# Layer 0 rotary embedding: even and odd head dimensions projected to separate tiles, in pairs

## The chip, the cores and the metric

The kernel runs on one core of a Trainium2 chip. The time is the device time of one launch in microseconds (us). TensorE is called PE in the profile (PEld is its weight loads), VectorE is DVE, ScalarE is ACT, GpSimd is POOL and SyncE is SP, which issues nearly all DMAs here.

## What is computed

Two transformer layers over 8 batch entries of 512 tokens by 256 channels. Layer 0 is causal attention with 16 heads of 16 dimensions and rotary position embedding, then a mixture of experts; layer 1 is a windowed attention and a second expert stage. The change touches only the queries and keys of layer 0:

```
q = shape_heads(x @ Wq.T)            # 16 heads of 16 dimensions
k = shape_heads(x @ Wk.T)
_rotate_every_two(x) = stack((-x_odd, x_even), -1).reshape(x.shape)
q = q * cos + _rotate_every_two(q) * sin
k = k * cos + _rotate_every_two(k) * sin
scores = einsum('bhqd,bhkd->bhqk', q, k) * scale      # causal mask, softmax, times v, Wo
```

The frequency of the rotation is the same for the two dimensions of a pair (even, odd), so `cos` and `sin` hold each value twice.

## The kernel before

Layer 0's attention is one function, `layer0_attention` (L246). What each engine does, and in which order, comes from one list of items that `schedule0` (L167) makes: each item is a kind of work, a batch entry `b` and indices, with a time key in units of one group of heads (4 heads; 4 groups to a batch entry, so entry `b` has its groups at 4b to 4b+3). The list is sorted by key, and every engine walks it and does its own kinds in that order; semaphores do the rest. A dictionary `SHIFTED` (L154) moves the keys of single kinds by hundredths of a group, and `front0` (L134) sets other keys for the first two batch entries.

The kinds that matter here:

- `qk` (PE, L395): one tile of a projection, 128 output channels by 512 tokens, from two fp32 chunks of 128 channels (four matmul records a tile). Four tiles of 128 channels hold q and k of a batch entry (i = 0, 1 for q, 2, 3 for k); each is projected twice, with the weights (j = 0) and with weights whose columns are swapped in pairs (j = 1), which gives the rotated partner. So a batch entry has 8 `qk` tiles.
- `rope` (DVE, L638): multiplies one `qk` tile in PSUM by a table (cos for j = 0, signed sin for j = 1) into `halves`, and frees the tile's PSUM bank. 8 a batch entry. `sum` (POOL, L795) adds the two halves.
- `hi` (ACT, L547), `rest` (DVE, L642), `mid` (POOL, L799), `lo` (DVE, L646) split the fp32 sum in three bf16 parts; `park` (SP, L353) writes these to DRAM, and `stack` (SP, L368) reads them back, six DMAs for q and six for k, in the layout in which the scores are made.
- `max` (PE L416 and L419, DVE L653): scores of a part of a group and their row maxima, 11 items a group, in three PSUM banks taken in turn: PE's item n waits until DVE has read item n-3.
- `split` (DVE, L663 to L668), `turn` (PE, L426), `turned` (ACT, L563), `send` (SP, L359): the maxima of a group are transposed and sent into the stacks.
- `exp` (PE L441 and L448, ACT L574): 10 items a group, in two banks. `values` (PE, L465): probabilities times v.
- Once a batch entry: `turn_o`, `norm`, `turn_a`, `out` (PE L499: output projection, two items), `add` (DVE L684), `stats` (DVE L689, L692), `new` (DVE L699), `turn_x` (PE L509), `v` (PE L402), `logit` (L518), `pick`, `rank`, `place`, `scatter` (POOL L815: four indirect DMAs).

`qk`, `turn`, `turn_o`, `turn_a`, `out`, `turn_x`, `v`, `logit` and `rank` share two PSUM banks (`Banks`, called `work`): an item takes the bank that was freed first, as the list has it, and PE waits until its last reader is done. Keys before the change, for entry b with g0 = 4b: tile i is projected at g0 - 7 + i + 0.08 (j = 0) and + 0.25 (j = 1), so each group has two `qk` items and their two `rope`s apart. `out` is at g0 + 5.50 and 5.62, `turn` 0.318 after each group's start, `new` at g0 + 6.06 and 6.24 and `turn_x` at 6.42. Of entry 1 the front has three of the four tiles; the fourth lies after the first maxima. Two `ones` items (DVE L611, L612) fill parts of the stacks before the first maxima.

At the start SP loads `w_qkv` (five blocks of 256 columns: q, k, q swapped, k swapped, v), the first x transposed, the rope table (two sets of channels, cos and sin) and the rest. After layer 0 come `experts` (L822) and layer 1, which start when layer 0 has ended.

Of the kernel before, what the change touches and what calls it, by code (L numbers as in the profile page):

```python
# [12 lines left out]
P = 128  # L13
# [120 lines left out]
def front0():  # L134


    time = {("xt", 1, 0, 0): -8.9, ("stack", 0, 0, 0): -6.52, ("stack", 0, 1, 0): -5.5}
    for i in range(4):
        t = -8 + 0.5 * i
        for j in range(2):  # L140
            time["qk", 0, i, j], time["rope", 0, i, j] = t + 0.2 * j, t + 0.1 + 0.2 * j
        for kind, late in (("sum", 0.35), ("hi", 0.36), ("rest", 0.85), ("mid", 0.9), ("lo", 0.93), ("park", 0.95)):
            time[kind, 0, i, 0] = t + late
        t = (-4.5, -4.0, -3.5, -1.0)[i]
# [10 lines left out]
    "add": {0: -0.032, 1: -0.093}, "exp": {None: -0.088}, "hi": {0: -0.04, 1: -0.079, 2: 0.027, 3: -0.079},  # L155
    "lo": {0: 0.197, 1: 0.34, 2: 0.033, 3: 0.228}, "logit": {None: 0.02}, "new": {0: -0.174, 1: -0.059},
    "norm": {0: -0.02, 1: -0.024, 2: 0.006, 3: -0.055}, "o_in": {None: -0.049}, "park": {2: 0.277},
    "qk": {(0, 0): 0.025, (0, 1): 0.025, (1, 0): 0.025, (1, 1): 0.025, (2, 0): 0.019, (2, 1): 0.08, (3, 0): -0.298, (3, 1): 0.025},
    "rest": {0: 0.006, 1: 0.109, 2: 0.166, 3: 0.2}, "rope": {(0, 0): -0.084, (0, 1): -0.099, (1, 0): -0.07, (3, 1): -0.103},
    "split": {None: 0.054}, "stats": {0: -0.063, 1: -0.067}, "sum": {0: -0.183, 1: -0.128, 2: -0.128, 3: -0.128},  # L160
    "turn": {None: 0.078}, "turn_a": {0: 0.097, 1: 0.024}, "turn_o": {0: 0.024, 1: 0.013, 2: 0.014, 3: -0.024},
# [5 lines left out]
def schedule0():  # L167
# [9 lines left out]
    for b in range(B):  # L177
        g0 = NG * b
        at(g0 - 9, "xt", b)
        for i in range(4):  # L180
            t = g0 - 7 + i
            for j in range(2):
                at(t + 0.08 + 0.17 * j, "qk", b, i, j)
# [1770 lines left out]
```

## Time and profile before

| what | value |
|---|---|
| time, median of 3 runs | 1361.81 us (1360.37 to 1361.99) |
| time of the profiled execution | 1357.76 us |
| its span, first to last instruction | 1356.0 us |
| mean granted TensorE clock | 0.969 |
| busy over the span | PE 1208.0, DVE 929.2, ACT 607.9, POOL 277.0 us |
| `qk` matmul records (L395) | 256, 64 tiles |

The span is the time between the first and the last instruction; what lies around it is 1.8 us here. A busy share is a mean over stages with different limits, so the windows by stage and by group say more. Overlapping records of one engine are merged in a busy time.

### The profile page before, as it was taken

To read this page: it belongs to the slowest core of one execution; us is meant where nothing else is said; L and a number is where in the kernel's file an instruction comes from. 1 tells how busy PE (TensorE), PEld (TensorE's weight loads), DVE (VectorE), ACT (ScalarE), POOL (GpSimd) and SP (SyncE) were. 2 spreads that over 40 slices of the span, in tenths; PEclk is the share of its full clock that TensorE was granted. 3 is DMA by queue.
4 is the path that set the end of the run, shared out by engine and by line. 5 is a ranking of instruction groups with operands and counts; after the bars stand their busy time and mean duration, and the time that the engine had idled before them with its cause. 6 is when DMAs were issued, how large, how long until landed. Compare 5 with 4: busy or idle time off the path is not lost. (4 is left out here: it accounts for less than half of the span.)

```text
span 1356.0 us, 32761 instructions
## 1 busy us (share of the span) xinstructions
PE 1208.0 (89%) x12587; PEld 779.8 (58%) x12641; DVE 929.2 (69%) x2335; ACT 607.9 (45%) x1144; POOL 277.0 (20%) x294
## 2 busy tenths in 40 slices
PE   7589999999999989779999778998989898989865
PEld 3245566655656555449998345555556565655542
DVE  3687767777686766237777668767776768676743
ACT  1044455555454556235554115554545454445441
POOL 3111121212121210111111411222222223212122
PEclk9689999999999999989999888999999999999998
DMA  5443524243342412544221344334251505140000
GB/s 181 129 121 96 148 72 118 80 110 103 87 130 60 130 47 98 186 134 153 71 68 36 95 135 120 98 75 118 57 138 39 148 28 150 38 123 3 19 17 16
DMA packets 68265, 127.88 MB, mean 94 GB/s; under 512 B 8320, under 2 KB 58128, under 8 KB 64656
## 3 DMA queue, kind: packets, MB, share of 16 engines
q1 hardware_dynamic: 65040, 117.38, 31.2%
q0 software_dynamic: 3072, 8.41, 1.9%
q8 instruction: 102, 1.67, 0.5%
q14 instruction: 51, 0.42, 0.1%
HBM read 84.31 MB, written 40.66 MB: 92 GB/s over the span
## 5 line engine op out<-in xcount | busy, mean ns | idle before, releaser
L574 ACT ACTIVATE arena<-pair 128x512 f32<-128x512 f32 x320 | 184.6, 596 | 112.4 <-PE pair L448 107.2
L1511 ACT ACTIVATE second_probs<-pair 128x512 f32<-128x512 f32 (+1 forms) x256 | 135.4, 541 | 195.7 <-PE pair L1373 159.2
L653 DVE TENSOR_REDUCE first_maxima<-bank 128x1 f32<-128x512 f32 (+3 forms) x235 | 146.8, 636 | 55.3 <-PE bank L419 54.5
L1671 DVE TENSOR_REDUCE second_maxima<-bank 128x3 f32<-128x480 f32 (+1 forms) x160 | 105.2, 660 | 58.9 <-PE bank L1340 56.8
L395 PE MATMUL bank<-first_xT,w_qkv 128*128 128x512 f32 x256 | 126.3, 624 | 12.1 <-DMA first_xT<-in_xT 7.9
L441 PE MATMUL pair<-stacks 128*128 128x128 bf16 (+3 forms) x458 | 102.4, 292 | 6.9 <-DMA stacks<-first_m_turned 5.6
L416 PE MATMUL bank<-stacks 96*128 96x512 bf16 (+3 forms) x343 | 87.3, 307 | 14.6 <-DVE first_maxima L653 11.5
L653 DVE TENSOR_REDUCE first_maxima<-pair 128x1 f32<-128x512 f32 (+3 forms) x117 | 74.6, 638 | 25.3 <-PE pair L419 24.8
L1365 PE MATMUL pair<-second_q_stack,second_k_stack 128*32 128x160 bf16 (+4 forms) x2048 | 83.3, 229 | 4.8 <-ACT second_probs L1511 2.8
L448 PE MATMUL pair<-constants_bf 128*128 128x256 bf16 (+1 forms) x320 | 80.7, 252 | 4.3 <-ACT arena L574 1.0
L795 POOL TENSOR_TENSOR first_halves<-first_halves 128x512 f32<-128x512 f32 x32 | 41.5, 1298 | 197.8 <-DVE first_halves L638 197.7
L395 PEld LDWEIGHTS bank<-first_xT,w_qkv 128*128 128x128 f32 x256 | 46.3, 198 | 57.5 <-issue 45.9
L875 PEld LDWEIGHTS pair<-expert_xsT,expert_W_near 128*128 128x128 f32 x624 | 75.5, 192 | 4.7 <-ACT expert_xsT L918 2.9
L875 PE MATMUL pair<-expert_xsT,expert_W_near 128*128 128x128 f32 x624 | 76.4, 276 | 1.8 <-ACT expert_xsT L918 1.8
L465 PE MATMUL pair<-arena,first_values 128*32 128x512 f32 (+3 forms) x1024 | 75.5, 436 | 0.7 <-ACT arena L574 0.7
L907 ACT ACTIVATE expert_W_near<-stacks 128x1024 f32 x39 | 41.1, 1056 | 76.5 <-PE pair L875 60.6
L886 PE MATMUL pair<-stacks,expert_hT 128*128 x312 | 73.9, 380 | 0.6 <-ACT expert_hT L922 0.6
L1365 PEld LDWEIGHTS pair<-second_q_stack,second_k_stack 128*32 128x32 bf16 x2048 | 42.2, 96 | 55.6 <-issue 45.0
L441 PEld LDWEIGHTS pair<-stacks 128*128 128x128 bf16 x512 | 42.3, 98 | 50.9 <-issue 18.2
L638 DVE TENSOR_TENSOR first_halves<-bank,rope 128x512 f32<-128x512 f32 x64 | 43.7, 685 | 34.2 <-PE bank L395 34.0
L1388 PE MATMUL pair<-second_probs,second_values 128*32 128x256 f32 (+1 forms) x1024 | 59.8, 354 | 3.0 <-ACT second_probs L1511 3.0
L886 PEld LDWEIGHTS pair<-stacks,expert_hT 128*128 128x128 f32 x312 | 56.2, 190 | 7.0 <-issue 1.0
(344 smaller groups left out, 2583.1 us busy)
## 6 DMA issues: line engine op xcount, KB each, us to landing
stacks<-parked SPq DMA_DIRECT2D x96, 256.0 KB, 5.2
parked<-first_parts SPq DMA_DIRECT2D x32, 384.0 KB, 2.8
second_q_stack<-parked SPq DMA_DIRECT2D x48, 256.0 KB, 5.0
second_k_stack<-parked SPq DMA_DIRECT2D x48, 256.0 KB, 8.2
parked<-second_parts SPq DMA_DIRECT2D x30, 384.0 KB, 2.6
expert_xs<-sorted_x SPq DMA_DIRECT2D x39, 128.5 KB, 2.1
sorted_y<-expert_ys SPq DMA_DIRECT2D x39, 128.0 KB, 1.7
first_xT<-in_xT SPq DMA_DIRECT2D x8, 512.0 KB
```

The lines of the kernel that those rows point to most:

```text
L395: ins = pe.matmul(bank[:, :], w["qkv0"][:, c, lo:lo + P], xT[b % 2][:, c, :], start=(c == 0), stop=(c == KC - 1))
L416: pe.matmul(mx[n % 3][:, x * wide:(x + 1) * wide], q[0:ROWS, i * GH + hh, qt * P:(qt + 1) * P], k[0:ROWS, i * GH + hh, 0:wide], start=(x = ...
L441: pe.matmul(ex[n % 2][:, lo:lo + wide], k[:, i * GH + hh, kt * P:(kt + 1) * P], q[:, i * GH + hh, kt * P:S], start=(lo == 0), stop=True, s ...
L448: ins = pe.matmul(o, m["idb"][:, :], spread(m["mT0"][:, :], P, len(heads) * len(tiles)), start=False, stop=True, skip_group_check=True)
L465: ins = pe.matmul(pv[VW * hh:VW * (hh + 1), kt * P:S], V[b % 2][:, kt, i * GH + hh, :], PT[:, slot(b, i, hh), lo:lo + S - kt * P], start=( ...
L574: act.activation(PT[:, s:s + len(heads), lo:lo + each], ex[n % 2][:, 0:len(heads) * each].rearrange("p (h q) -> p h q", h=len(heads)), ACT ...
L653: dve.tensor_reduce(nm[:, i, qt, heads[0]:heads[0] + len(heads)], mx[n % 3][:, 0:wide].rearrange("p (h k) -> p h k", h=len(heads)), AX.X, ...
L875: last = pe.matmul(pair[0][:, (j % 2) * F + n * P:(j % 2) * F + (n + 1) * P], near[:, j % 2, c, n * P:(n + 1) * P], xsT[:, j % 2, c * P:(c ...
L886: last = pe.matmul(pair[1][:, (j % 2) * F:(j % 2) * F + D], hT[:, j % 2, c, :], W2[:, c, bass.ts(e, D)], start=(c == 0), stop=(c == FC - 1))
L1365: pe.matmul(ex[n % 2][s * SUB:(s + 1) * SUB, lo:lo + wide], k[:, h, k0:k0 + SUB], q[:, h, k0:k0 + wide], start=(y == 0), stop=True, skip_g ...
L1511: act.activation(PT[:, s:s + len(heads), lo:lo + each], scores[:, :, 0:each], ACT.Exp, scale=SCALE).then_inc(lp["exps"], 1)
L1671: dve.tensor_reduce(nm[:, i, :, :].rearrange("p t h -> p (t h)")[:, first:end], mx[n % 2][:, 0:(end - first) * wide].rearrange("p (u k) -> ...
```

## The change

Weights are ordered so that the even dimensions of all heads (128 channels) make one tile and the odd dimensions the other. A pair of tiles, E and O, gives both rotated halves: E cos - O sin and O cos + E sin. The swapped projections go: `w_qkv` has three blocks instead of five, the rope table is half as large, and a batch entry has four `qk` tiles, not eight. The number of `rope`, `sum`, `hi`, `rest`, `mid`, `lo`, `park` and `stack` items stays. Each tile is now read by two `rope`s; the banks of a pair are freed by the third and fourth `rope` of the pair, which are in the order E cos, O sin, E sin, O cos. Pairs stand at g0 - 6.7 (q) and g0 - 4.7 (k), that is in every second group; the first `sum` chain of a pair follows it, the second is 0.6 of a group later. All `SHIFTED` entries of `qk`, `rope`, `sum`, `hi`, `rest`, `lo` and `park` are dropped. In the front both pairs of entry 1 lie ahead of the first maxima.

```diff
-    for i in range(4):
-        t = -8 + 0.5 * i
...
+    for p in range(2):
+        t = -8 + 0.75 * p
+        for n in range(2):
+            time["qk", 0, 2 * p + n, 0] = t + 0.1 * n - 0.15 * p
+            for j in range(2):
+                time["rope", 0, 2 * p + n, j] = t + 0.2 + 0.1 * n + 0.04 * (j if n == 0 else 1 - j)
...
+        t = (-4.4, -3.3)[p]
...
-        for i in range(4):
-            t = g0 - 7 + i
-            for j in range(2):
-                at(t + 0.08 + 0.17 * j, "qk", b, i, j)
-            for j in range(2):
-                at(t + 0.21 + 0.17 * j, "rope", b, i, j)
-            for n, kind in enumerate(("sum", "hi", "rest", "mid", "lo", "park")):
-                at(t + 0.44 + 0.09 * n, kind, b, i)
+        for p in range(2):
+            t = g0 - 6.7 + 2 * p
+            for n in range(2):
+                at(t + 0.04 * n, "qk", b, 2 * p + n)
+                for j in range(2):
+                    at(t + 0.08 + 0.06 * n + 0.03 * (j if n == 0 else 1 - j), "rope", b, 2 * p + n, j)
+                for q, kind in enumerate(("sum", "hi", "rest", "mid", "lo", "park")):
+                    at(t + 0.21 + 0.6 * n + 0.09 * q, kind, b, 2 * p + n)
...
         if kind == "rope":
-            return [("qk", b, i, j)]
+            return [("qk", b, i - j, 0)] if i % 2 else []
...
-                        dve.wait_ge(lp["qk_ps"], 2 * k + j + 1)
-                        if k >= 2 and j == 0:
+                        of = i ^ j
+                        dve.wait_ge(lp["qk_ps"], 4 * b + of + 1)
+                        if k >= 2:
                             dve.wait_ge(lp["lo"], k - 1)
-                        bank, before = work["qk", b, i, j]
-                        dve.tensor_tensor(halves[:, k % 2, j, :], wk[bank][:, :], w["rope"][:, i % 2, j, :], ALU.mult)\
-                            .then_inc(read[bank], 1)
+                        bank, before = work["qk", b, of, 0]
+                        dve.tensor_tensor(halves[:, k % 2, j, :], wk[bank][:, :], w["rope"][:, j, :], ALU.mult)\
+                            .then_inc(read[bank] if i % 2 else lp["roped"], 1)
...
-                        is_read(pool, ("qk", b, i, 0))
-                        is_read(pool, ("qk", b, i, 1))
-                        pool.tensor_tensor(halves[:, k % 2, 0, :], halves[:, k % 2, 0, :], halves[:, k % 2, 1, :], ALU.add)\
+                        if i % 2:
+                            is_read(pool, ("qk", b, i - 1, 0))
+                            is_read(pool, ("qk", b, i, 0))
+                        else:
+                            pool.wait_ge(lp["roped"], k + 2)
+                        pool.tensor_tensor(halves[:, k % 2, 0, :], halves[:, k % 2, 0, :], halves[:, k % 2, 1, :],
+                                           ALU.add if i % 2 else ALU.subtract)\
...
-                w = {"qkv0": si("w_qkv0", [P, KC, 5 * D]), "o0": si("w_o0", [P, KC, D]), "rope": si("rope", [P, 2, 2, S]),
+                w = {"qkv0": si("w_qkv0", [P, KC, 3 * D]), "o0": si("w_o0", [P, KC, D]), "rope": si("rope", [P, 2, S]),
```

## Rows read from the trace of the kernel before

**Rows 1.** Windows: length, busy us (count) of PE, PEld, DVE, ACT, POOL, PEclk, DMA share, GB/s.

```profile
57.30:73.90 16.60, 14.78 (x61) 6.43 (x62) 12.93 (x29) 1.22 (x2) 1.26 (x1) 0.71 0.18 58
73.90:131.00 57.10, 53.46 (x363) 29.24 (x368) 45.51 (x88) 28.81 (x52) 6.27 (x7) 0.94 0.42 109
...
195.30:259.50 64.20, 63.15 (x467) 38.06 (x473) 47.91 (x117) 32.68 (x60) 12.55 (x13) 1.00 0.37 100
```

**Rows 2.** Windows of the four groups of one period, from one group's first `exp`.

```profile
195.30:208.90 13.60, 13.55 (x118) 8.52 (x118) 11.61 (x28) 8.36 (x16) 1.28 (x1) 1.00 0.31 88
208.90:225.40 16.50, 16.12 (x112) 9.62 (x113) 11.57 (x24) 7.78 (x14) 2.50 (x3) 1.00 0.68 169
225.40:244.30 18.90, 18.74 (x136) 12.39 (x138) 12.45 (x34) 8.93 (x16) 2.94 (x3) 1.00 0.07 23
244.30:259.50 15.20, 14.74 (x105) 7.53 (x106) 12.28 (x34) 7.61 (x15) 5.83 (x6) 1.00 0.45 131
```

**Rows 3.** Timeline of PE: start, length, engine, line, tiles, count.

```profile
206.07 0.33 PE L416 MATMUL bank<-stacks 96*128 96x384 bf16 x1
...
206.62 0.39 PE L416 MATMUL bank<-stacks 96*128 96x256 bf16 x2
...
246.09 1.93 PE L395 MATMUL bank<-first_xT,w_qkv 128*128 128x512 f32 x4
247.86 0.38 PE L441 MATMUL pair<-stacks 128*128 128x512 bf16 x1
```

**Rows 4.** Timeline of DVE: two instructions without a wait between them.

```profile
209.59 0.69 DVE L653 TENSOR_REDUCE first_maxima<-bank 128x4 f32<-128x512 f32 x1
210.20 0.68 DVE L646 TENSOR_TENSOR first_parts<-first_halves,first_parts 128x512 bf16<-128x512 f32 x1
```

**Rows 5.** Timeline of the front, PE and DVE.

```profile
7.86 12.59 PE L395 MATMUL bank<-first_xT,w_qkv 128*128 128x512 f32 x24 [7.86 <-DMA first_xT<-in_xT]
...
47.01 3.47 DVE L611 MEMSET stacks<- 32x4096 int32 x1 [0.91 <-issue]
...
47.95 0.38 PE L416 MATMUL bank<-stacks 96*128 96x512 bf16 x1 [3.01 <-DMA stacks<-parked]
...
54.79 0.14 DVE L620 TENSOR_SCALAR arena<-arena 8x1 f32<-8x1 f32 x1
...
57.31 1.28 DVE L653 TENSOR_REDUCE first_maxima<-bank 128x1 f32<-128x512 f32 x2
```

**Rows 6.** Issues of DMAs: KB each, us to landing.

```profile
w_qkv<-in_qkv SPq DMA_DIRECT2D x1, 1280.0 KB, 5.6
...
rope<-in_rope SPq DMA_DIRECT2D x1, 1024.0 KB, 8.5
```

**Rows 7.** Timeline of SP: the last park of entry 0 and the stack of k.

```profile
31.64 1.11 SPq L353 DMA_DIRECT2D parked<-first_parts  x2
38.74 3.65 SPq L368 DMA_DIRECT2D stacks<-parked  x6
```

**Rows 8.** Windows: the first 8 us, and two stretches with a less busy PE.

```profile
0.00:8.00 8.00, 0.14 (x1) 0.18 (x2) 0.07 (x1) 1.28 (x1) 2.46 (x10) 1.00 0.78 293
...
74.00:86.00 12.00, 10.03 (x62) 5.78 (x63) 10.89 (x23) 6.45 (x12) 0.62 (x1) 0.74 0.49 135
476.00:510.00 34.00, 28.38 (x249) 18.49 (x252) 22.93 (x63) 18.09 (x34) 4.98 (x5) 1.00 0.20 52
```

**Rows 9.** Timeline of DVE in the maxima ahead of the first group.

```profile
67.37 0.69 DVE L653 TENSOR_REDUCE first_maxima<-bank 128x1 f32<-128x512 f32 x1 [1.85 <-PE bank L419]
...
70.11 0.69 DVE L653 TENSOR_REDUCE first_maxima<-pair 128x1 f32<-128x512 f32 x1 [0.86 <-PE pair L419]
```

**Rows 10.** Timeline, second and third group of a period: ACT and PE.

```profile
217.60 0.59 ACT L563 ACTIVATE first_m_turned<-bank 12x512 bf16<-12x512 bf16 x1 [1.68 <-PE bank L426]
...
234.85 0.63 PE L509 MATMUL bank<-constants,first_x 128*128 128x128 f32 x4
```

**Rows 11.** Page, costliest groups: count, busy us, mean ns, idle before it.

```profile
L795 POOL TENSOR_TENSOR first_halves<-first_halves 128x512 f32<-128x512 f32 x32 | 41.5, 1298 | 197.8 <-DVE first_halves L638 197.7
```

More of the change, by code:

```diff
@@ L134, in front0 @@
 def front0():
-    time = {("xt", 1, 0, 0): -8.9, ("stack", 0, 0, 0): -6.52, ("stack", 0, 1, 0): -5.5}
-    for i in range(4):
-        t = -8 + 0.5 * i
-        for j in range(2):
[L141 to L144, printed above, removed]
-        for j in range(2):
-            time["qk", 1, i, j], time["rope", 1, i, j] = t + 0.1 + 0.17 * j, t + 0.23 + 0.17 * j
-        for n, kind in enumerate(("sum", "hi", "rest", "mid", "lo", "park")):
-            time[kind, 1, i, 0] = t + 0.46 + 0.09 * n
+    time = {("xt", 1, 0, 0): -8.9, ("stack", 0, 0, 0): -7.25, ("stack", 0, 1, 0): -6.5}
+    for p in range(2):
[4 more added lines that the diff above has]
+                time["rope", 0, 2 * p + n, j] = t + 0.2 + 0.1 * n + 0.04 * (j if n == 0 else 1 - j)
+            for kind, late in (("sum", 0.36), ("hi", 0.37), ("rest", 0.5), ("mid", 0.52), ("lo", 0.55), ("park", 0.57)):
+                time[kind, 0, 2 * p + n, 0] = t + late + 0.12 * n
+        t = (-4.4, -3.3)[p]
+        for n in range(2):
+            time["qk", 1, 2 * p + n, 0] = t + 0.04 * n
+            for j in range(2):
+                time["rope", 1, 2 * p + n, j] = t + 0.08 + 0.06 * n + 0.03 * (j if n == 0 else 1 - j)
+            for m, kind in enumerate(("sum", "hi", "rest", "mid", "lo", "park")):
+                time[kind, 1, 2 * p + n, 0] = t + 0.21 + 0.3 * n + 0.06 * m
     for i in range(2):
@@ L154 @@
 SHIFTED = {
[L155 to L161, printed above, removed]
+    "add": {0: -0.032, 1: -0.093}, "exp": {None: -0.088},     "logit": {None: 0.02}, "new": {0: -0.174, 1: -0.059},
+    "norm": {0: -0.02, 1: -0.024, 2: 0.006, 3: -0.055}, "o_in": {None: -0.049},             "split": {None: 0.054}, "stats": {0: -0.063, 1: -0.067},     "turn": {None: 0.078}, "turn_a": {0: 0.097, 1: 0.024}, "turn_o": {0: 0.024, 1: 0.013, 2: 0.014, 3: -0.024},
     "turn_x": {1: 0.012}, "turned": {None: 0.006}, "v": {0: -0.023, 1: 0.069}, "v_in": {1: 0.029}, "values": {0: 0.037},
@@ L179, in schedule0 @@
         at(g0 - 9, "xt", b)
[L180 to L187 removed]
+        for p in range(2):
+            t = g0 - 6.7 + 2 * p
+            for n in range(2):
+                at(t + 0.04 * n, "qk", b, 2 * p + n)
+                for j in range(2):
+                    at(t + 0.08 + 0.06 * n + 0.03 * (j if n == 0 else 1 - j), "rope", b, 2 * p + n, j)
+                for q, kind in enumerate(("sum", "hi", "rest", "mid", "lo", "park")):
+                    at(t + 0.21 + 0.6 * n + 0.09 * q, kind, b, 2 * p + n)
         for i in range(2):
@@ L1924, in rope_tables @@
     inv = (1.0 / 10000.0 ** (np.arange(0, HD, 2, dtype=np.float32) / np.float32(HD))).astype(np.float32)
-    ang = np.repeat(np.arange(S, dtype=np.float32)[:, None] * inv[None, :], 2, axis=-1)
-    sign = np.where(np.arange(HD) % 2 == 0, -1.0, 1.0)
-    both = np.stack([np.cos(ang), np.sin(ang) * sign], 0).transpose(2, 0, 1)
-    return np.ascontiguousarray(np.repeat(both, H, 0).reshape(2, P, 2, S).transpose(1, 0, 2, 3).astype(np.float32))
+    ang = np.arange(S, dtype=np.float32)[:, None] * inv[None, :]
+    both = np.stack([np.cos(ang), np.sin(ang)], 0).transpose(2, 0, 1)
+    return np.ascontiguousarray(np.repeat(both, H, 0).astype(np.float32))
 def kernel(**x):
```

15 lines of the change are left out of this document (7 added, 8 removed).

## The prediction

> **What bounds the kernel now.** I read the windows by stage first, then the windows of the single groups, then the timelines of PE and DVE where the projections lie. The chain of waits on the page reaches back only into layer 1, so it says nothing of layer 0; but the experts start when layer 0 has ended, so every us that layer 0 loses or gains is one of the whole. After the ramp, layer 0 runs in periods of 64.2 us, one a batch entry, with PE busy 63.15, DVE 47.91 and ACT 32.68 us [rows 1]. The reader is to see that PE has no gap in any of the four groups, 0.4 us at most [rows 2], and that what follows a projection starts the moment its stream is through: a tile's four records take from 246.09 to 247.86, 1.77 us start to start [rows 3]. So PE sets the pace there. In the 16.6 us ahead of the first `exp` it does not: the clock is at 0.71 and DVE, with 12.93 us, carries the maxima [rows 1]. Before that, the first reduction starts at 57.31, after DVE's memsets (47.01 to 54.79) and a last `rest` and `lo`; PE had its stacks at 47.95 and waited for DVE [rows 5].
>
> **What the change removes, as PE alone has it.** Behind the first maxima lie the 8 tiles of each of entries 2 to 7 and the 2 of entry 1's fourth, 50 in all; afterwards there are 24, 4 for each of six entries. The 26 tiles that go are 46 us at 1.77 us each. That is the most this part can give, if the rest of the work can be fed as fast. I do not expect it, since DVE keeps all its work: 47.91 us in a period whose PE work falls by 4 x 1.77 = 7.1 to 57.1 us is 84%, and its place in the period changes.
>
> **The front.** w_qkv falls from 1280 to 768 KB and the rope table from 1024 to 512 KB [rows 6]. 0.52 MB less ahead of the first matmul at 293 GB/s [rows 8] is 1.8 us: PE starts near 6.1, not 7.86 [rows 5]. Then I followed the new order with DVE at 0.6 us an instruction (209.59 to 210.20, [rows 4]), POOL's sum at 1.3 [rows 11], ACT's and POOL's casts at 0.6 as ACT's copy of one bank [rows 10]. Pair q: E done at 9.5, O at 11.8, four `rope`s until 13.8, `lo` of both at 16.8 and 18.9. Pair k: projected meanwhile, `rope`s 18.9 to 21.3, last `lo` 26.6, where the last park of entry 0 was issued near 32 before. With the 7.1 us from park to stack, 31.64 to 38.74, and the 9.2 from there to PE's first score at 47.95 [rows 5, 7], the k stack is there at 43. DVE: entry 1's first pair ends at 36.4, second pair's `rope`s at 38.9, memsets (7.8) until 47, the two `rest` and `lo` of the second pair until 51.5. So DVE is still what is late, and the maxima start at 51.5 against 57.3: **-5.8 us** (bounds: -1.8, the start alone, and -14, if the k stack alone set it).
>
> **The maxima ahead of the first group** lose the fourth tile of entry 1, which lay between them twice at half clock: 1.85 and 0.86 us of DVE's waits [rows 9], and two `rope`s, a `rest` and a `lo` at 0.6. That is 5.1 us; some of it hides another wait, I take **-4.3** (bounds -2.4 and -5.1).
>
> **The period, group by group.** Per group, the keys leave these tiles: first group 0 (one before), second 2 (2), third 0 (2), fourth 2 (3). On PE alone that makes 13.6, 16.5, 18.9, 15.2 [rows 2] into 11.8, 16.5, 15.4 and 13.4. DVE's four instructions a tile, 2.4 us in every group before, become 1.2, 3.6, 1.2, 3.6: 10.4, 12.8, 11.3 and 13.5 from the busy times of rows 2. So in the fourth group DVE needs as much as PE has, and I walked both lists through the three maxima banks:
> - *Fourth group.* The `turn` lies between the two projections and the second one takes its bank: PE waits 0.25 for ACT's copy of 0.59 [rows 10]. DVE waits for O, then has four `rope`s, `rest` and `lo` between maxima of 0.5 to 0.6, while PE makes a `max` and an `exp` in 0.55, 206.07 to 206.62 [rows 3]. DVE falls 3 to 4 us behind, the three banks hide about half. PE loses 0.25 + 1.75 us here and in the start of the first group; `values` (PE only) lets DVE catch up.
> - *First group.* `turn_o` and `turn_a` wait 0.35 us for `norm`, which now has a `lo` ahead of it.
> - *Second group.* Key 5.50 of the older entry, `out`, comes 0.16 of a group after O. Both shared banks are held until the third `rope`: O sin, a maximum and E sin are 0.12 + 0.6 + 0.5 + 0.7, 1.9 us after O's end; PE has one `max` and one `exp`, 0.5 us, in the meantime. It waits 1.4, with the `turn` 1.6 us. `max` and `exp` behind it in PE's list wait too.
> - *Third group.* No projection is left to cover the chain `stats`, `split`, `new`. `turn_x`, which waits for it, came 9.5 us into the group, at 234.85 [rows 10]. DVE enters 1.2 us later (`rest` and `lo` of q fell into the group before), and saves a `rope` and a `lo`: `turn_x` comes at 8.4. PE's own work ahead of it would let it come at 6.2, so 2.2 of the 3.5 us are not gained.
>
> Sum: waits of 2.0 + 0.35 + 1.6 + 2.2 = 6.1 against 7.1 removed. PE idled 64.2 - 63.15 = 1.05 us a period before [rows 1]; 0.8 of it lies where the new waits are and is no longer added. That makes 1.8 us a period, 62.4 against 64.2. Bounds: -7.1 (no new wait) and +2 (each wait half again as long, and none of the old gaps swallowed). Five such periods: **-9.0 us**. SP's parks come earlier in the period than before, no DMA is added, and `hi` stands 0.13 of a group, 2 us, behind the last `rope`, longer than the sum of 1.3: I cost these at nothing. If the sum came later, behind the four indirect DMAs in POOL's list, ACT would hold up the `exp`s by the difference; the bound of +2 holds 1 us of that.
>
> **The ramp**, 57.1 us [rows 1], five groups without `out`, `stats` and `logit` in most: -1.0 (a `rest` and a `lo` gone from a DVE-bound group), +0.5, -3.1 (two tiles gone, no `new` to wait for), -1.2, -0.85: **-5.7** (bounds -9 and -2). From 476 us on no tile is projected and nothing changes.
>
> **Sum**: 5.8 + 4.3 + 9.0 + 5.7 = 24.8 us. The profiled execution was 1357.76, so 1333.0; the median lies 4.05 higher, so 1337.0 us.
>
> **Two rules weighed.** That PE is the bound rests here on matmul busy time, and on start-to-start times beside it. The Trainium skill (Perfetto Trace Analysis, Identifying the Most-Contended Engine) warns of the first: matmuls are pipelined, so weight load busy is the better measure. By that measure PE is at 38.06 of 64.2 us, 59%. The starts that follow each other at once speak against reading it as room [rows 1, 3]. If it were room, the tiles would buy nothing in the period, and the time would be that of the second rival below.
>
> Where PE gets gaps its clock can fall. It was granted 0.74 over 12 us with PE busy 10.03, and 1.00 over 34 us with 28.38 [rows 8], about the same share. A period of 62.4 us with some 57 us of work lies above both. The Trainium skill (TensorE: Matmul & The Clock Gate, The HAM clock gate) has activity open the gate and idle time close it, and the trace agrees in the front.
>
> **Rivals.**
> - *All of it is gained.* DVE has 9 us of room in a period and PE stays full: 5.8 + 4.3 + 24 x 1.77 = 52.6, so 1309 us (1300 to 1322). For it: DVE idles 16 us in a period now. Against: it idles in other places. 20%.
> - *Only the front.* PE was not the bound in the period, or the waits eat all 7.1 us: 10.1 us and little of the ramp, 1351 (1347 to 1359). 8%.
> - *The clock falls* in each period for a stretch of 6.8 us, which costs 3.4: 5 x 3.4 = 17, so 1354. 7%.
> - *Slower.* The held banks: if DVE comes to the third `rope` with a backlog, `out` waits far longer, and PE's list behind it. It decides from 1.6 + 24.8 / 6 = 5.7 us a period on, seven more DVE instructions ahead; at 6.5 us it is 1337 + 29 = 1366. Against: DVE waits for O just before, so its queue is empty there. 8%.
> - No change that shows: 4%, for example the same with a 5.5 us wait.
>
> My own case, 1322 to 1347, has 53%. A change under 0.2% (2.7 us) is about what cannot be told from none. Faster: 53 + 20 + 8 + 7 = 88%, same 4, slower 8. The range reaches down over two thirds of the full gain, to 1306, and up over the front-only and the clock cases, to 1355.
>
> **What would show it.** First x waits until about 6; first reduction at 51 to 52; first `exp` near 64; a period of 62 to 63 us whose PE busy is near 57; PE's idle time ahead of L499 ended by DVE's `rope`, 1.4 us in each period, and ahead of the transpose of x by `new`; DVE over 75% busy. A period of 57 would prove me wrong in the waits, one over 64 in the bound; an unchanged start of the maxima in the front.

## The result: slower by 0.6%, and the profile after

The changed kernel takes 1370.33 us (median; 1364.23 to 1373.66) against 1361.57 (1358.71 to 1363.52): a ratio of 1.0062, 95% interval [1.0044, 1.008]. I had forecast 1337, with 0.88 for faster and 1355 as the upper end. The profiled execution took 1366.95 us with a span of 1365.2, 9.2 us more than before.

From the page of the changed kernel, the totals and the projections:

```profile
PE 1171.4 (86%) x12513; PEld 760.5 (56%) x12513; DVE 937.2 (69%) x2335; ACT 607.9 (45%) x1144; POOL 276.3 (20%) x294
...
L394 PE MATMUL bank<-first_xT,w_qkv 128*128 128x512 f32 x128 | 63.5, 625 | 9.6 <-DMA first_xT<-in_xT 6.8
```

The projections have half their records (128 for 256), and PE is 36.6 us less busy. The work did go; PE stands idle in its place. Lines of the changed file: `qk` L394, `max` L415 and L418, `exp` L440, `values` L464, `turn_o` L473, `out` L498, `turn_x` L508, `hi` L546, `sum` L798, `mid` L803; DVE's numbers stayed.

Windows of the changed kernel, columns as in [rows 1]: first the stages of layer 0 from one group's first `exp` to another's, then the maxima ahead of the first group, then the four groups of one period and their sum:

```profile
0.00:69.60 69.60, 36.04 (x107) 17.11 (x108) 44.19 (x71) 8.11 (x12) 18.02 (x27) 0.77 0.48 142
69.60:126.30 56.70, 50.42 (x358) 27.82 (x356) 44.29 (x85) 28.98 (x52) 5.21 (x6) 0.92 0.35 88
126.30:165.60 39.30, 31.53 (x227) 18.27 (x226) 23.98 (x52) 15.94 (x29) 3.96 (x5) 0.91 0.74 166
165.60:474.10 308.50, 273.73 (x2173) 164.97 (x2172) 233.34 (x559) 155.67 (x283) 60.94 (x64) 1.00 0.34 94
...
57.07:69.60 12.53, 11.32 (x53) 4.88 (x54) 12.20 (x29) 0.59 (x1) 0.00 (x0) 0.64 0.28 80
264.00:278.30 14.30, 12.34 (x115) 7.84 (x114) 12.83 (x30) 8.43 (x16) 2.29 (x3) 1.00 0.52 137
278.30:296.20 17.90, 16.46 (x115) 9.66 (x114) 11.22 (x23) 7.49 (x14) 1.75 (x2) 1.00 0.60 144
296.20:314.80 18.60, 15.86 (x131) 10.88 (x130) 13.44 (x34) 8.99 (x17) 3.03 (x4) 1.00 0.21 72
314.80:329.30 14.50, 13.42 (x104) 6.54 (x102) 11.44 (x33) 7.75 (x15) 5.44 (x6) 1.00 0.11 38
264.00:329.30 65.30, 58.07 (x459) 34.92 (x457) 48.93 (x117) 32.65 (x60) 12.52 (x14) 1.00 0.36 98
```

The same stages of the kernel before, as far as [rows 1] does not have them:

```profile
131.00:161.20 30.20, 29.78 (x229) 18.21 (x231) 23.27 (x51) 16.21 (x29) 3.78 (x4) 1.00 0.78 191
161.20:465.40 304.20, 299.49 (x2219) 180.98 (x2251) 228.28 (x558) 155.84 (x282) 60.37 (x62) 1.00 0.35 95
```

| stage | before | after | difference |
|---|---|---|---|
| up to the first reduction | 57.3 | 57.1 | -0.2 |
| maxima, up to the first `exp` | 16.6 | 12.5 | -4.1 |
| first four groups | 57.1 | 56.7 | -0.4 |
| next two groups | 30.2 | 39.3 | **+9.1** |
| the following 19 groups | 304.2 | 308.5 | **+4.3** |
| what is left (1356.0 - 465.4; 1365.2 - 474.1) | 890.6 | 891.1 | +0.5 |

So there are two losses, one that happens once and one of every period: 65.3 us where it was 64.2. PE is busy 58.07 us of it, 5.1 less than before (7.1 us of projections were taken out; no run separates the other 2.0), and idles 7.2 us instead of 1.05. The timeline of PE in the changed kernel shows where: from 262 to 316 us it has nine idle times, 7.05 us together, of which these are four (in brackets the idle time ahead of the instruction and what ended it):

```profile
266.88 0.39 PE L415 MATMUL pair<-stacks 96*128 96x512 bf16 x1 [1.14 <-DVE first_maxima L653]
...
289.78 1.97 PE L498 MATMUL bank<-w_o,first_attendedT 128*128 128x256 f32 x8 [1.44 <-DVE first_halves L638]
...
298.77 0.39 PE L415 MATMUL bank<-stacks 96*128 96x512 bf16 x1 [1.07 <-DVE first_maxima L653]
...
305.44 0.66 PE L508 MATMUL bank<-constants,first_x 128*128 128x128 f32 x4 [0.85 <-DVE first_x L699]
```

All nine are ended by DVE, which is busy 75% of the period (48.93 of 65.3): five by a reduction, one each by `norm` (0.78), a rope (1.44), `new` (0.85) and `rank`'s input (0.41). DVE has a quarter of the period to spare, so my reading was that PE waits for DVE's *order*, for one instruction that stands behind something longer; runs 2, 3 and 7 to 9 test it.

One such instruction is `lo`, and it has grown. Groups of DVE in the changed kernel and in the one before:

```profile
L646 DVE TENSOR_TENSOR first_parts<-first_halves,first_parts 128x512 bf16<-128x512 f32 x32 | 33.9, 1060 | 5.9 <-POOL first_parts L803 5.9
```

```profile
L646 DVE TENSOR_TENSOR first_parts<-first_halves,first_parts 128x512 bf16<-128x512 f32 x32 | 21.9, 685 | 11.3 <-POOL first_parts L799 11.1
```

32 instructions each; the mean went from 685 to 1060 ns. 14 of the 32 take 1.5 us or more, the others 0.69 as before. A long one looks like this (timeline of DVE, then of POOL, changed kernel):

```profile
264.70 1.51 DVE L646 TENSOR_TENSOR first_parts<-first_halves,first_parts 128x512 bf16<-128x512 f32 x1
```

```profile
263.81 0.62 POOL L803 TENSOR_SCALAR first_parts<-first_halves 128x512 bf16<-128x512 f32 x1 [1.92 <-DVE first_halves L642]
264.40 1.27 POOL L798 TENSOR_TENSOR first_halves<-first_halves 128x512 f32<-128x512 f32 x1
```

POOL does the `mid` of one tile and at once the `sum` of the next, and DVE's `lo` of the first tile runs beside that `sum`: 1.51 us instead of 0.68. The Trainium skill (SBUF — State Buffer, SBUF: two separate sides) says that a DVE operation with two SBUF inputs and a GpSimd operation that reads SBUF lock each other out of a port pair. The trace agrees: both inputs of `lo` are in SBUF. When this `lo` starts, 0.97 us of the `sum` are left, and it takes 0.83 us more than alone; the `lo` at 53.14 in the front starts with 1.19 us left and takes 1.06 more. Of the DVE instructions in layer 0 that run beside a `sum`, only those with two inputs in SBUF are long, all of them: 14 `lo` and 2 `rest`. The 31 `rope`s beside a `sum` (one input in PSUM) take 0.68 us as always, and the reductions, whose one input is in PSUM, are as short as before (635 ns in the mean, 636 before).

In the kernel before, the same pair met three times in the front in the other order, DVE's `rest` first. There DVE is as short as ever and the `sum` is the long one, 1.57 to 1.58 us instead of 1.27. Timelines of DVE and POOL, kernel before:

```profile
17.66 0.68 DVE L642 TENSOR_TENSOR first_halves<-first_halves,first_parts 128x512 f32<-128x512 f32 x1
```

```profile
17.89 1.58 POOL L795 TENSOR_TENSOR first_halves<-first_halves 128x512 f32<-128x512 f32 x1 [2.16 <-DVE first_halves L638]
```

So in both kernels the one that starts second pays.

### The profile page after: what moved, and what is told of

It reads as the page before. It is cut to its first block and busy times, and to the rows that moved or that the text cites. A ratio compares the mean times of both kernels' runs of the same rounds, so it can differ in the third digit from the quotient of the medians.

```text
span 1365.2 us, 32573 instructions
## 1 busy us (share of the span) xinstructions
PE 1171.4 (86%) x12513; PEld 760.5 (56%) x12513; DVE 937.2 (69%) x2335; ACT 607.9 (45%) x1144; POOL 276.3 (20%) x294
## 5 line engine op out<-in xcount | busy, mean ns | idle before, releaser
L440 PE MATMUL pair<-stacks 128*128 128x512 bf16 (+3 forms) x512 | 124.5, 305 | 9.6 <-DMA stacks<-first_m_turned 8.0
L415 PE MATMUL bank<-stacks 96*128 96x512 bf16 (+3 forms) x343 | 89.4, 314 | 34.4 <-DVE first_maxima L653 28.3
L464 PE MATMUL pair<-arena,first_values 128*32 128x512 f32 (+3 forms) x1024 | 76.4, 439 | 0.7 <-ACT arena L573 0.7
L798 POOL TENSOR_TENSOR first_halves<-first_halves 128x512 f32<-128x512 f32 x32 | 40.6, 1269 | 157.8 <-DVE first_halves L638 157.2
L394 PE MATMUL bank<-first_xT,w_qkv 128*128 128x512 f32 x128 | 63.5, 625 | 9.6 <-DMA first_xT<-in_xT 6.8
L440 PEld LDWEIGHTS pair<-stacks 128*128 128x128 bf16 x512 | 42.2, 99 | 44.6 <-ACT arena L573 9.3
L415 PEld LDWEIGHTS bank<-stacks 96*128 96x128 bf16 x343 | 31.5, 101 | 63.6 <-DVE first_maxima L653 39.9
L418 PE MATMUL bank<-constants_bf 128*128 128x128 bf16 (+2 forms) x235 | 59.7, 254 | 0.0
```

The lines of the kernel that those rows point to most:

```text
L415: pe.matmul(mx[n % 3][:, x * wide:(x + 1) * wide], q[0:ROWS, i * GH + hh, qt * P:(qt + 1) * P], k[0:ROWS, i * GH + hh, 0:wide], start=(x = ...
L440: pe.matmul(ex[n % 2][:, lo:lo + wide], k[:, i * GH + hh, kt * P:(kt + 1) * P], q[:, i * GH + hh, kt * P:S], start=(lo == 0), stop=True, s ...
L464: ins = pe.matmul(pv[VW * hh:VW * (hh + 1), kt * P:S], V[b % 2][:, kt, i * GH + hh, :], PT[:, slot(b, i, hh), lo:lo + S - kt * P], start=( ...
```

## The experiments

The theory when they were made: the tiles that went were worth their time (PE was the bound), and what took it back is four places of the new order, each with its own price. The main rival was that the removed PE work was never worth anything, because DVE or the exchange by DMA sets the period. Each run is compared with runs of the kernel before on the same chip: medians 1362.02 for the first four, 1362.64 for the next four, 1361.68 for the last two. "Against the changed kernel" is a difference of medians to 1370.33, from a series of its own; my estimate from the intervals is that it is uncertain by some 3 us. The profiled executions add a spread of their own: what lies behind the 25th group, where nothing is projected any more, took 890 to 897 us in them. The stages and periods of layer 0 are therefore the finer measure.

**1. Was PE the bound?** The kernel before, with the swapped projections made from one of their two chunks of 128 channels; the other half of these products is left out, all else stays.

```diff
-                        for c in range(KC):
+                        for c in range(KC - j):
...
-                                            start=(c == 0), stop=(c == KC - 1))
+                                            start=(c == 0), stop=(c == KC - 1 - j))
```

> The kernel before, in its own order, but each swapped projection (j = 1) is made from one of its two chunks of channels, so half of its matmuls are left out and the rotated halves are not the true ones. This takes 4 x 0.88 = 3.5 us of PE out of each period and moves nothing else. Theory A (PE set the pace before, and the new order's waits ate the gain): the period falls from 64.1 us by 2.5 to 3.5, and the whole by 15 to 22 us. Theory B (PE was not the bound, its busy time only looked full): less than 1 us a period and less than 5 us of the whole.

1342.72 us (1342.19 to 1346.02), ratio 0.9865 [0.9846, 0.9884]: 19.3 us faster. Window of one period:

```profile
248.00:308.90 60.90, 60.12 (x466) 36.49 (x465) 48.04 (x116) 32.66 (x60) 12.49 (x13) 1.00 0.40 106
```

This period is 60.9 us, 3.3 less, for 4 x 1.77 / 2 = 3.5 us of PE work taken out. It is the best one: others are 61 to 62 us, and the 19 groups that took 304.2 us take 291.1, so 2.8 us a period, four fifths of the work taken out. PE was the bound, with DVE and the DMAs as they were. This settles the main rival: the removed work had its value, and the new order took it away. It also sets aside the reading by weight load busy (59%) that I had weighed in the prediction.

**2. Order of the ropes.** Changed kernel, ropes E cos, E sin, O sin, O cos: the first bank is free after the second rope, not the third.

```diff
-                    at(t + 0.08 + 0.06 * n + 0.03 * (j if n == 0 else 1 - j), "rope", b, 2 * p + n, j)
+                    at(t + 0.08 + 0.03 * n + 0.06 * (j if n == 0 else 1 - j), "rope", b, 2 * p + n, j)
```

> The changed kernel with the four ropes of each steady pair in the order E cos, E sin, O sin, O cos: the bank of E is free before O is projected, and DVE has work in the 0.99 us in which it waited for O. Theory A (the held banks and DVE's bunched work cost the time): PE's wait of 1.44 us ahead of the output projection goes in each of 5 to 6 periods, and some of the waits for maxima; the whole falls by 6 to 12 us against the changed kernel. Rival (DVE's total work in the period is the bound, so a wait that goes comes back later): less than 3 us. Rival (the time is lost in the front and in one stall of the DMAs): no change.

1363.36 us (1357.31 to 1369.31), ratio 1.0012 [0.9996, 1.0027]; 7.0 us less than the changed kernel. Windows of the second group and of the third group of two periods, then the timeline of PE at `out`:

```profile
275.40:291.70 16.30, 16.30 (x115) 9.67 (x114) 11.25 (x23) 7.51 (x14) 1.74 (x2) 1.00 0.65 157
291.70:311.90 20.20, 17.46 (x131) 12.09 (x130) 13.47 (x34) 9.15 (x17) 3.04 (x4) 0.92 0.22 66
...
227.80:246.40 18.60, 15.85 (x130) 10.88 (x129) 13.44 (x34) 9.02 (x17) 3.07 (x4) 1.00 0.24 72
```

```profile
285.31 1.95 PE L498 MATMUL bank<-w_o,first_attendedT 128*128 128x256 f32 x8
```

The second group is 16.3 us instead of 17.9, full to the last tenth, and `out` follows with no idle time. The fourth group is 15.2 instead of 14.5: here ACT stands in `hi` 1.12 us for POOL's `sum` (0.45 in the changed kernel), which needs O sin and so starts only behind the third rope. And the third group has two lengths, 18.6 and 20.2; I come to that.

**3. The sum beside `lo`.** Changed kernel, the second `sum` of a pair right behind the first, so that POOL has none to do beside `lo`.

```diff
-                    at(t + 0.21 + 0.6 * n + 0.09 * q, kind, b, 2 * p + n)
+                    at(t + 0.21 + (0.01 if kind == "sum" else 0.6) * n + 0.09 * q, kind, b, 2 * p + n)
```

> The changed kernel with POOL's second sum of each steady pair right behind the first, not behind the cast (mid) of the first. In the changed kernel that sum starts as DVE starts lo, and lo takes 1.51 us, not 0.68, 14 times. Theory: two operations with two SBUF inputs each, one on DVE and one on POOL, hold each other up; apart, lo falls back to 0.68 to 0.70 in the steady periods, DVE gains 0.83 us twice a period, and the whole falls by 3 to 8 us. Rival: lo is long because its input from the cast comes late, or for another reason of its own, and it stays at 1.5. Second rival: it gets short, but lies off the path, and the time stays within 2 us.

1366.3 us (1360.07 to 1368.58), ratio 1.0025 [1.0013, 1.0037]; 4.0 us less. Groups of DVE in this kernel:

```profile
L642 DVE TENSOR_TENSOR first_halves<-first_halves,first_parts 128x512 f32<-128x512 f32 x32 | 25.7, 804 | 2.9 <-ACT first_parts L546 2.6
L646 DVE TENSOR_TENSOR first_parts<-first_halves,first_parts 128x512 bf16<-128x512 f32 x32 | 23.9, 748 | 5.9 <-POOL first_parts L803 5.9
```

`lo` is back at 748 ns; only in the front two long ones are left. Moving nothing but the `sum` did it, which is what a shared port asks for and a slower DVE would not. Nine `rest`s now meet it instead (1.11 us; the mean of `rest` is 804 ns, 709 in the changed kernel). The third group falls from 18.6 to 17.8 and the first from 14.3 to 13.9 where the clock stays up.

**4. The one-off stall.** SP's queue, changed kernel:

```profile
128.53 0.37 SPq L352 DMA_DIRECT2D parked<-first_parts  x1
128.94 0.49 SPq L332 DMA_DIRECT2D b<-in_b1T  x1
...
130.08 0.67 SPq L335 DMA_DIRECT2D sorted_x<-first_zero  x1
...
133.57 1.94 SPq L358 DMA_DIRECT2D stacks<-first_m_turned  x3
```

SP's queue, kernel before:

```profile
124.05 1.82 SPq L359 DMA_DIRECT2D stacks<-first_m_turned  x3
125.92 0.43 SPq L333 DMA_DIRECT2D b<-in_b1T  x1
...
138.58 1.93 SPq L359 DMA_DIRECT2D stacks<-first_m_turned  x3
```

PE, changed kernel, where it waits for that `send`:

```profile
144.87 0.61 PE L440 MATMUL pair<-stacks 128*128 128x512 bf16 x1 [4.36 <-DMA stacks<-first_m_turned]
```

The kind `biases` (three loads and a zero fill, once) has key 4.0. Before, the park of tile 2 of entry 2 had key 4.167, behind it; now it has 3.96, and SP waits in it for DVE's `lo`. The bulk transfers start at 128.94 instead of 125.92, and while before the next `send` came 12 us behind them, it is now 2.8 us behind the zero fill; its three small DMAs land late and the `exp`s of the next group wait for them. Around this wait, from 143.6 to 150.4 us, the granted clock is 0.50. The experiment puts `biases` ahead of that park:

```diff
-    at(NG, "biases", 0)
+    at(3.5, "biases", 0)
```

> The changed kernel with the biases item (a 1 MB load, a 0.9 MB clear of DRAM and a small one, all on SP's queue) at key 3.5 instead of 4.0, so ahead of the park that now stands at 3.96. In the changed kernel these transfers went out at 129 us, and the sends and the park behind them took 9 and 12 us to land; the fifth and sixth group took 39.4 us against 30.2 before. Theory: their place behind a park that waits for DVE makes that stall; the two groups fall to 32 or less and the whole by 5 to 8 us. Rival: the park and the k stack of entry 2 are slow for themselves (six loads of 256 KB in front of them in each period), and the two groups stay above 37.

1366.22 us (1358.02 to 1369.11), ratio 1.0022 [1.0005, 1.004]; 4.1 us less. Window of the two groups:

```profile
124.00:156.20 32.20, 28.80 (x227) 17.48 (x226) 24.05 (x52) 15.92 (x29) 4.04 (x5) 1.00 0.74 177
```

32.2 us instead of 39.3, at full clock: the stall is gone, 7.1 us. The other 2.0 of the 9.1 us are not the stall's. Of the 7.1 only 4.1 reach the median, and the profiled execution (1367.19 us) is not shorter at all. It gains another 2.3 us ahead of these two groups, but loses 3.3 us in two third groups at half clock, and 6.1 us behind layer 0's last projections, where the code is the same:

```profile
468.20:1365.40 897.20, 786.01 (x9652) 534.59 (x9649) 591.16 (x1573) 398.87 (x771) 187.80 (x194) 0.96 0.30 85
```

That stage took 891.1 us at a clock of 0.97 in the changed kernel. Why its clock differs from one execution to the next stays open.

**5. The three together**, edits as above.

> The changed kernel with the three edits tried alone (rope order, second sum early, biases early) together. If each took away a wait of its own, they add: the period from 65.3 to about 62.7 us (first group 13.4 to 13.9, second 16.3, third 17.8, fourth 14.5 to 15.2), the fifth and sixth group from 39.4 to about 31, the whole near 1352 to 1356 us. If they only move one backlog of DVE, they give no more than the best of them, about 1363.

1354.38 us (1349.67 to 1356.59), ratio 0.9932 [0.9914, 0.9951]. That is 15.9 us less than the changed kernel; the three alone were 7.0 + 4.0 + 4.1 = 15.1. With an uncertainty of 3 us in each that alone would prove little, but the periods say the same: without a stretch at half clock one is 65.3 us in the changed kernel, 63.9 in run 2, 64.1 in run 3 and 62.6 here, so 1.4 and 1.2 alone and 2.7 together. The causes are separate and they add up. With them the change is a gain of 0.7%.

**6. The front.** Timeline of DVE in the changed kernel ahead of the first reduction, then POOL's:

```profile
43.45 3.47 DVE L610 MEMSET stacks<- 32x4096 int32 x1 [0.91 <-issue]
...
51.73 0.67 DVE L642 TENSOR_TENSOR first_halves<-first_halves,first_parts 128x512 f32<-128x512 f32 x1
53.14 1.74 DVE L646 TENSOR_TENSOR first_parts<-first_halves,first_parts 128x512 bf16<-128x512 f32 x1 [0.74 <-POOL first_parts L803]
...
57.07 1.28 DVE L653 TENSOR_REDUCE first_maxima<-bank 128x1 f32<-128x512 f32 x2
```

```profile
52.48 0.62 POOL L803 TENSOR_SCALAR first_parts<-first_halves 128x512 bf16<-128x512 f32 x1 [9.79 <-DVE first_halves L642]
53.07 1.26 POOL L798 TENSOR_TENSOR first_halves<-first_halves 128x512 f32<-128x512 f32 x1
```

The chain is to be read across the engines. DVE's memsets hold the first `rest` until 51.73; POOL's list has `mid` of that tile ahead of the `sum` of the next, so this `sum` stands 9.8 us and runs at 53.07, beside `lo` (1.74 us); `hi`, `rest`, `mid` and `lo` of the second tile come behind it, all in front of the first reduction. The list itself asks for this: it puts the second tile's `sum` at 0.51 of a group, behind the first's `lo` at 0.45. The edit, on top of run 5, gives both tiles of entry 1's pairs their steps side by side:

```diff
-                time[kind, 1, 2 * p + n, 0] = t + 0.21 + 0.3 * n + 0.06 * m
+                time[kind, 1, 2 * p + n, 0] = t + 0.21 + 0.01 * n + 0.06 * m
```

> As c3, and in the front the second tile's chain of entry 1 (sum, hi, rest, mid, lo) directly beside the first's instead of behind it. In the changed kernel DVE's two memsets stand between the last ropes and the first rest, POOL's last sum stands behind the cast that waits for this rest, and the first reduction comes at 57.1 us, not 51.5 as forecast. Theory: the serial chain behind the memsets costs it; the first reduction comes 2.5 to 3 us earlier, and the whole by as much. Rival: the park of the tile before holds it (ACT waited for a park's landing at 43.4), then nothing moves.

1350.05 us (1347.37 to 1353.75), ratio 0.9908 [0.9893, 0.9923]; 4.3 less than run 5. Timeline of DVE in this kernel:

```profile
51.84 1.69 DVE L646 TENSOR_TENSOR first_parts<-first_halves,first_parts 128x512 bf16<-128x512 f32 x2 [0.52 <-POOL first_parts L803]
53.45 1.27 DVE L653 TENSOR_REDUCE first_maxima<-bank 128x1 f32<-128x512 f32 x2
```

The first reduction comes at 53.45 (56.63 in run 5).

In the third group this kernel, too, has two lengths. Windows of it in two periods, and PE at the transposes of x in the longer one:

```profile
279.10:296.90 17.80, 15.71 (x128) 10.89 (x130) 12.64 (x34) 8.99 (x17) 1.80 (x3) 1.00 0.22 75
341.70:361.10 19.40, 17.15 (x127) 12.12 (x129) 12.62 (x34) 9.16 (x17) 1.82 (x3) 0.91 0.19 68
```

```profile
350.16 1.12 PE L508 MATMUL bank<-constants,first_x 128*128 128x128 f32 x4 [0.85 <-DVE first_x L699]
```

Same instructions, same waits, 1.6 us more: from about 350 on TensorE runs at the lower of its two levels, 1.2 GHz instead of 2.4, and the four transposes of x take 1.12 us where they take 0.66 in the changed kernel. What PE did before it: from 347 on it waited for DVE 0.21, 0.47 and 0.85 us between short pieces. The waits alone do not decide it: the changed kernel has them too (0.21, 0.47 and 0.85, and 1.07 ahead of them) in every period. Between 155 and 455 us the profiled executions of the changed kernel, of runs 2 to 4 and of runs 5 and 6 have 0, 2, 3, 2, 4 and 4 such stretches.

**7 and 8. The chains behind what PE waits for.** If it is DVE's order that matters, `rest` and `lo` of a tile must not stand ahead of `new` (third group) or `norm` (first group). They are not urgent, since the stacks are read over a group later. On top of run 6, a table of how late each step of a chain is, per pair and tile (`sum`, `hi`, `rest`, `mid`, `lo`, `park`); run 7 moves the chains of the q pair behind `new`:

```diff
+CHAIN = (((0.21, 0.3, 1.12, 1.17, 1.32, 1.34), (0.22, 0.9, 1.22, 1.27, 1.44, 1.46)),
+         ((0.21, 0.3, 0.39, 0.48, 0.57, 0.66), (0.22, 0.9, 0.99, 1.08, 1.17, 1.26)))
...
-                for q, kind in enumerate(("sum", "hi", "rest", "mid", "lo", "park")):
-                    at(t + 0.21 + (0.01 if kind == "sum" else 0.6) * n + 0.09 * q, kind, b, 2 * p + n)
+                for kind, late in zip(("sum", "hi", "rest", "mid", "lo", "park"), CHAIN[p][n]):
+                    at(t + late, kind, b, 2 * p + n)
```

> As c4, and rest, mid, lo and park of both q tiles of a steady pair 0.7 and 0.2 of a group later, into the second half of the third group, where DVE idles 5 us. The number of instructions stays. Theory A: the first half of the third group is a stretch that DVE bounds (PE waited 1.07, 0.21, 0.47 and 0.85 us there, and TensorE's clock falls there in some periods and runs, 1.6 us each time); the third group falls from 17.8 to about 16, the dips of the clock go, the whole falls by 8 to 14 us. Rival: the chain of stats, split and new sets this stretch by itself, and the third group loses less than 0.5 us.

1338.1 us (1336.03 to 1341.04), ratio 0.9829 [0.9816, 0.9843]; 12.0 less than run 6. Window of a third group:

```profile
275.30:292.00 16.70, 15.37 (x127) 10.90 (x129) 12.89 (x34) 8.91 (x17) 2.28 (x3) 1.00 0.20 59
```

16.7 us in every period, from 17.8 or 19.4. PE's waits there are down to 0.33 and 0.85 us, and no stretch at the lower clock is left in the periods: 5 x 1.1 for the wait and 4 x 1.6 for the clock make 11.9. Run 8 moves the second k tile behind `norm` as well: its `rest`, `mid`, `lo` and `park` at 1.42, 1.46, 1.58 and 1.60.

> As c5, and rest, mid, lo and park of the second k tile 0.4 of a group later, behind the four norms of the first group. Theory: PE's wait of 0.78 us for norm goes, 0.5 to 1 us a period, 3 to 6 us of the whole. Rival: the k stack then comes later and the maxima wait for it, so the second or fourth group grows by as much or more.

1333.1 us (1332.3 to 1335.43), ratio 0.9788 [0.9775, 0.98]; 5.0 less than run 7. Window of a first group and ACT's timeline at the end of a fourth:

```profile
240.80:253.30 12.50, 12.14 (x114) 7.82 (x113) 11.41 (x28) 8.45 (x16) 0.81 (x2) 1.00 0.49 134
```

```profile
299.40 0.63 ACT L550 ACTIVATE first_parts<-first_halves 128x512 bf16<-128x512 f32 x1 [1.12 <-POOL first_halves L802]
```

The first group is 12.5 us, 13.4 in run 7. Next in line is ACT: `hi` of the first k tile waits 1.12 us for a `sum`, with the `exp`s behind it. The `sum` in turn waits for DVE, for the third rope of the pair, and not for the indirect DMAs ahead of it in POOL's list, which had been done 0.84 us before:

```profile
298.11 1.27 POOL L802 TENSOR_TENSOR first_halves<-first_halves 128x512 f32<-128x512 f32 x1 [0.84 <-DVE first_halves L642]
```

**9. The late chains alone.** Only this step on the changed kernel, with the sums, ropes and `biases` where they were, to see that it doesn't need the others.

```diff
+CHAIN = (((0.21, 0.3, 1.12, 1.17, 1.32, 1.34), (0.81, 0.9, 1.22, 1.27, 1.44, 1.46)),
+         ((0.21, 0.3, 0.39, 0.48, 0.57, 0.66), (0.81, 0.9, 1.42, 1.46, 1.58, 1.6)))
```

> The changed kernel with only the chains of the q tiles and of the second k tile later (as in c6), the rope order, the place of the sums, of the biases and the front as in the changed kernel. Theory A (in the steady periods most of the loss is where DVE's rest and lo stand, and TensorE's clock falls only because of these waits): the third group falls from 18.6 to about 17, the first from 14.3 to about 13, no half-clock stretch is left between 165 and 455 us, lo of q is short (its sum is long done), and the whole falls by 12 to 18 us against the changed kernel, to about 1355. Rival (the held banks and the biases carry most): less than 8 us. If c5's and c6's gain needs the rope order to be in place first, it falls by less than the 17 us that both gave on top of c4.

1352.42 us (1347.19 to 1355.5), ratio 0.9935 [0.9913, 0.9958]; 17.9 less than the changed kernel, the largest of the single steps, though the one-off stall is still in it. It is not the order alone: one `lo` a period, that of q, is short again as well (the mean of `lo` is 904 ns, from 1060). With that settled beforehand, from run 6 to run 8, the late chains gave 17.0 us, of which some 6 are the clock's. One period and its third group:

```profile
256.80:319.30 62.50, 57.25 (x452) 34.98 (x457) 48.40 (x117) 32.59 (x60) 12.54 (x14) 1.00 0.38 103
288.00:304.80 16.80, 15.46 (x128) 10.95 (x130) 12.98 (x35) 8.98 (x17) 2.28 (x3) 1.00 0.20 57
```

**10. ACT's wait.** Run 8 with the first k tile's `hi`, `rest`, `mid`, `lo` and `park` at 0.42, 0.49, 0.55, 0.64 and 0.68 (0.3, 0.39, 0.48, 0.57 and 0.66 before).

> As c6, and the first k tile's hi 0.12 of a group later, with rest, mid and lo 0.07 to 0.1 later. In c6 PE waits 0.93 us in the fourth group for an exp of ACT, which stands behind that hi, and the hi for a sum that starts only with the third rope. Theory: the hi holds ACT up; the wait goes, the fourth group falls from 15.17 by 0.7 to 1.0 us, the whole by 3 to 6 us. Rival: DVE's backlog sets this stretch, and the wait comes back at the next maximum; less than 1.5 us of the whole.

1325.4 us (1322.48 to 1327.02), ratio 0.9731 [0.9707, 0.9754]; 7.7 less than run 8. One period:

```profile
239.10:298.50 59.40, 56.95 (x451) 34.98 (x457) 47.61 (x117) 32.52 (x60) 12.44 (x13) 1.00 0.40 108
```

59.4 us, with PE idle 2.4. The fourth group fell from 15.2 to 14.6, for a forecast of 0.7 to 1.0, and the first, of which I had said nothing, from 12.5 to 11.8. This version keeps the change and is 2.7% faster than the kernel before. The kernel before has keys set one by one in `SHIFTED`, which the change dropped for these kinds; whether it would gain by the placements of runs 2 to 10 too was not tried. In its periods PE idles 1.05 us, so there is little to win there, but its front waits for DVE as well.

## Why the prediction was wrong

The step that failed is the walk of DVE's list against PE's: it priced DVE's work at 0.6 us an instruction wherever it stood, put the place of the second `sum` and of the parks at nothing, and so had the waits of a period at 6.1 us, less 0.8. By the groups' lengths they are 8.2.

What held: PE was the bound, and work taken from it is worth about four fifths of its length (run 1; I had taken all of it). The gap of the fourth group in [rows 2] is 0.46 us, not 0.4 at most, which changes nothing. The maxima ahead of the first group took 12.5 us, 4.1 less, for a forecast of 4.3. `out` waits 1.44 us for DVE's rope in the second group, for a forecast of 1.4 (run 2 takes it away), and the transpose of x waits for `new`: it comes 9.2 us into the third group, for a forecast of 8.4. My sign for being wrong in the bound, a period over 64 us, came (65.3), yet run 1 shows the bound to be right: a long period can also mean more waits, and the sign did not tell these apart.

What failed, by the steps of the sum:

- **The period, -1.8 us forecast, +1.1 measured.** PE's own work and the waits I listed were 12.15 us in the first group, 18.1 in the second, 17.6 in the third and 15.4 in the fourth, less 0.8 that I took off for old gaps. Measured: 14.3, 17.9, 18.6 and 14.5. The second is right. First and fourth together are 1.2 us over, the third 1.0, and the 0.8 was not there to be taken off. By group, what the forecast had as waits and what the lengths leave above PE's own work are 0.35 and 2.5 us, 1.6 and 1.4, 2.2 and 3.2, 2.0 and 1.1: the largest miss is in the first group. One part is the count of DVE's work at 0.6 us an instruction. In the first and the third group a `lo` takes 1.5 us because POOL's `sum` of the next tile, 0.6 of a group later, runs beside it. I had looked at that `sum` only as something that ACT might wait for, and costed it at nothing. The rest is that I priced each wait from DVE's load in a group (my walk of both lists), where what counts is which single instruction stands ahead of a reduction, `norm` or `new`. Run 3 has the share of the long `lo`, 1.2 us a period; runs 7 and 8 have the order's, 2.0 us a period on top of runs 5 and 6, without the clock.
- **The ramp, -5.7 forecast for five groups.** The 57.1 us that I took for five groups are four; without the fifth the forecast is -4.8. These four gave 0.4, and behind them lies the loss of 9.1 us, 7.1 of it the stall of run 4. "SP's parks come earlier in the period than before [...] I cost these at nothing" was the wrong zero. Earlier in the list is not earlier in time: a park whose key moved ahead of a one-off bulk load made SP wait in it, and the load slid against a small urgent transfer. Run 4 shows it.
- **The front, -5.8 forecast, -0.2 measured.** The k stack was there at 42.6, for a forecast of 43, and DVE was what was late, as I said. PE's start came 1.0 us earlier (6.85), not 1.8. But entry 1's first pair was through at 39.9, not 36.4, since its projection stands behind `v` in PE's list (PE at 28.03 behind 6.5 us of L401), and the memsets ended at 51.2, not 47. Behind them stood a chain over POOL and ACT, 5.3 us, where I had counted DVE's four instructions with short gaps. Run 6 takes 3.2 us out of it.
- **The clock rival** (7%) did not come in the profiled execution: it has no stretch at the lower clock in the steady periods. The run times of this kernel go with its mean clock (1364 to 1369 us at 0.961 to 0.965, 1370 to 1374 at 0.955 to 0.958), and the profiled one is 3.4 us below the median. Two such stretches as in runs 2 to 6 would explain that, but so would the stage behind layer 0, which varied by up to 7 us over the profiled executions; neither is shown.

The slower case that I had named, an `out` held by a backlog at the banks, did not occur. Stage by stage, with the forecast in the table's stages, the miss is 5.6 us in the front, 0.2 in the maxima, 4.4 in the first four groups, 10.4 in the next two (-1.3 forecast), 12.9 in the following 19 (-8.6 forecast) and 0.5 in what is left: 34.0 us, what lies between the 1333.0 forecast for the profiled execution and its 1366.95. None of it needs the change's arithmetic: with the same tiles and another order of the list, run 10 is 45 us below the median of this kernel.

Left open: at 59.4 us the period of run 10 is still 2.3 us above the 57.1 that PE alone would have; half of that is the wait for `new` (0.85) and `rank` (0.41). What makes the clock fall in one period and not in the next, with the same waits, stays open.

## What to carry to other kernels

When work is taken from the bound engine in a list-ordered kernel, the gain can go to whatever stands ahead of that engine's next input on the second engine. Walk, instruction by instruction, what precedes each value that the bound engine waits for, and put all that is not urgent behind it; here that step was worth 17.9 us on the changed kernel. Look in every list for what a moved item now stands in front of, one-off items too, and at what runs *beside* each long DVE instruction with two SBUF inputs.

## What the runs showed of the hardware

- A DVE `TENSOR_TENSOR` on 128x512 fp32 with both inputs in SBUF took 1.51 us, up to 1.74, instead of 0.68 when a POOL `TENSOR_TENSOR` of 1.27 us had started before it. In the other order, DVE first, it took 0.68 and POOL's took 1.57 to 1.58 (three times in the kernel before). DVE instructions with one input in PSUM (31 `rope`s, 24 reductions) were not longer beside it. Moving the POOL instruction alone restored it (run 3).
- TensorE's granted clock fell to 1.2 GHz after idle times of 0.21, 0.47 and 0.85 us in four of five periods with the same instructions and the same waits (runs 5 and 6), which cost 1.6 us each; in the fifth, and in all periods of the changed kernel's profiled execution, it did not fall with these waits. It stayed at 2.4 GHz in all steady periods once the waits were fewer (0.33 and 0.85 us, run 7; runs 8 to 10 likewise). The Trainium skill (TensorE: Matmul & The Clock Gate, The HAM clock gate) has idle time close the gate. In the steady periods it fell only behind such waits, as the page has it; these 1.5 us of waits did not always close it, and cost 3.1 when they did.
- Three small transfers (4 KB each) issued behind 1.9 MB on the same queue were waited for until 9 us after the last was issued: `send` was issued from 133.57 to 135.51 and PE went on at 144.87, with the DMA engines busy 0.91 of the time from 126.3 to 144.9.
